# Attention's values divided by VectorE out of PSUM, in two halves of a pair

## The reference

```python
qkvg = x @ w_attn                                  # q 16 heads, k 8, v 8, gate 8
log_g = log_sigmoid(6.906768 + qkvg[..., QKV:])
q = _rope(q); k = _rope(k); k = repeat(k, 2); v = repeat(v, 2)
log_G = repeat(cumsum(log_g, axis=1), 2)
s = einsum('bthd,bshd->bhts', q, k) * scale
logits = 2 * log(abs(s) + 1e-30) + log_G[:, :, :, None] - log_G[:, :, None, :]
logits = where(tril, logits, -inf)
m = max(logits, axis=-1)
a = where(tril, exp(logits - m), 0)
num = einsum('bhts,bshd->bthd', a, v)
den = sum(a, axis=-1)
y = num / (den[..., None] + 1e-06)
y = (y - mean(y)) / sqrt(var(y) + 1e-09) * ln_w    # over the 64 of a head
attn = y.reshape(B, T, hq * d) @ w_proj
```

## Time and profile before

| | |
|---|---|
| median of 3 runs | 1180.68 us (1180.38 to 1182.2) |
| profiled execution | 1181.45 us, span 1179.7 us |
| busy: TensorE, VectorE, ScalarE, GpSimd | 1085.6, 927.7, 768.3, 678.2 us |
| mean granted TensorE clock | 0.984 of full speed |

### The profile page before, as it was taken

How to read it: one execution, slowest core, us unless ns; L and a number is a source line. 1 busy time by engine, 2 the same in 40 slices (tenths; PEclk the granted TensorE clock), 3 DMA queues, 4 the chain that set the end, 5 groups by cost and what they waited for, 6 DMA issues and landing times.

```text
span 1179.7 us, 23035 instructions
## 1 busy us (share of the span) xinstructions
PE 1085.6 (92%) x8367; PEld 790.3 (67%) x8367; DVE 927.7 (79%) x2046; ACT 768.3 (65%) x1630; POOL 678.2 (57%) x828
## 2 busy tenths in 40 slices
PE   3998788899999999999999999999999998999894
PEld 2665556566666777676767777777767676767663
DVE  6755856887878787878777787978798899998882
ACT  1323446676777786868687777877776677677751
POOL 0240508898988554554636373736577777877531
PEclk9999999999999999999999999999999999999997
DMA  8000101111111102020201111111111111112100
GB/s 226 1 1 1 31 10 51 38 33 32 30 29 45 44 22 74 19 77 19 68 26 43 36 53 44 53 44 28 36 43 42 53 53 49 53 35 68 35 8 18
DMA packets 40080, 49.33 MB, mean 42 GB/s; under 512 B 5631, under 2 KB 28157, under 8 KB 39968
## 3 DMA queue, kind: packets, MB, share of 16 engines
q1 hardware_dynamic: 35872, 42.33, 12.7%
q0 software_dynamic: 4096, 5.54, 1.7%
HBM read 33.15 MB, written 9.18 MB: 36 GB/s over the span
## 4 chain that ended last, share of the span: by engine, by line
PE 62%; POOL 16%; DVE 12%; issue 8%; ACT 1%; DMA 0%; POOLq 0%; SPq 0%; DVEq 0%; ACTq 0%
PE P L674 15%; PE P L644 15%; PE P L552 5%; POOL xe_d L1406 4%; PE P L605 4%; PE P L621 3%; POOL U L1353 3%; PE P L580 3%; PE P L595 2%; POOL U L1357 2%; POOL U L1399 2%; PE P L487 2%; PE P L490 2%; PE P L499 2%; PE P L587 2%
## 5 line engine op out<-in xcount | busy, mean ns | idle before, releaser
L644 PE MATMUL P<-Qt,Kt 64*128 64x256 f32 (+1 forms) x2560 | 293.9, 368 | 0.6 <-DVE U L1221 0.6
L644 PEld LDWEIGHTS P<-Qt,Kt 64*128 64x128 f32 x2560 | 218.7, 186 | 72.5 <-issue 53.8
L838 ACT ACTIVATE U<-P 128x512 f32<-128x512 f32 x384 | 207.5, 595 | 33.0 <-PE P L644 33.0
L674 PE MATMUL P<-U 128*64 128x256 f32 (+1 forms) x1792 | 195.0, 357 | 0.0
L835 ACT ACTIVATE U<-U 128x384 f32<-128x384 f32 x256 | 122.8, 524 | 70.9 <-DVE U L1221 70.8
L1221 DVE SCALAR_TENSOR_TENSOR U<-P,U 128x384 f32<-128x384 f32 x256 | 128.8, 550 | 49.4 <-PE P L644 42.4
L674 PEld LDWEIGHTS P<-U 128*64 128x64 f32 x1792 | 113.1, 137 | 69.4 <-issue 26.0
L1353 POOL TENSOR_TENSOR U<-U,consts 128x192 f32<-128x192 f32 x136 | 81.6, 623 | 131.1 <-ACT U L768 127.7
L1357 POOL TENSOR_TENSOR U<-U 128x384 f32<-128x384 f32 x128 | 134.3, 1049 | 35.2 <-DVE U L1204 19.3
L1251 DVE SCALAR_TENSOR_TENSOR P<-U,ES,P 128x512 f32<-128x512 f32 x192 | 144.3, 751 | 5.2
L1399 POOL TENSOR_TENSOR U<-U,SM 128x1024 f32<-128x1024 f32 x32 | 74.7, 2335 | 123.9 <-DVE SM L1285 123.7
(11 more groups left out here) (180 smaller groups left out, 2042.4 us busy)
## 6 DMA issues: line engine op xcount, KB each, us to landing
U<-H_d SPq DMA_DIRECT2D x32, 512.0 KB, 3.8
Kt<-Kt SPq DMA_DIRECT2D x64, 128.0 KB, 2.3
U<-in_w SPq DMA_DIRECT2D x21, 256.0 KB, 3.2
acc<-in_x SPq DMA_DIRECT2D x4, 512.0 KB, 5.9
out<-acc SPq DMA_DIRECT2D x8, 256.0 KB, 2.8
xe_d<-U SPq DMA_DIRECT2D x3, 448.0 KB, 7.0
U<-xe_d SPq DMA_DIRECT2D x7, 192.0 KB, 3.4
ye_d<-U SPq DMA_DIRECT2D x7, 192.0 KB, 5.1
```

The source lines that it names most:

```text
L644: mm = te.matmul(bank[:, 256 * n:256 * n + 256 - lo], Kt[u % 2][ki][rows, 128 * j:128 * j + 128], Qt[w // 2][rows, 256 * (w % 2) + lo:256 ...
L674: mm = te.matmul(P[3][64 * hd:64 * hd + 64, c + lo:c + 256], vt, A[s % NA][:, o:o + 256 - lo], start=i == 0 and n == 0, stop=i == m and n ...
L838: s.activation(A[n % NA][:, 512 * hd:512 * hd + 512], P[BANK["score", n, hd]][:, :], ACT.Square, scale=0.125, bias=GUARD).then_inc(a_sq, 1)
```

## The change

The quotient moves to VectorE and is made for each half of a pair as soon as its transposes are in PSUM. `quotient(p, i)` waits for the transposes, makes 1e-6 M + denominator for 8 columns straight out of PSUM, its reciprocals, and the product of the bank (128x512) with them, broadcast over 64 columns, into Y. ScalarE's copy (`y` in `ACT_AT`), VectorE's `sum` and GpSimd's `n1` are gone. The bank of `y` is free when the product is there (v_y instead of a_y); `ysq` waits for v_y of both halves. The wait for the transposes of the pair before last (p_fin), which protects Y, moves from ScalarE to VectorE. All four tables have new ticks.

```diff
--- before.py
+++ after.py
@@ -39,31 +39,31 @@
 FIRST = {154: ("proj", 0, 0), 158: ("proj", 0, 1), 162: ("proj", 0, 2), 166: ("proj", 0, 3),
          170: ("proj", 0, 4), 174: ("k", 0, 0), 175: ("proj", 0, 5), 179: ("proj", 0, 6), 181: ("q", 0, 0),
          183: ("proj", 0, 7), 188: ("k", 0, 1)}
-PE_AT = [(6.83, "max", 0), (12.46, "max", 1), (18.06, "max", 2), (23.8, "max", 3), (19.46, "y", 0), (24, "y", 1),
-         (39.58, "fin", 0), (39.63, "fin", 1), (49.26, "wp", 0), (51.14, "wp", 1), (-10.47, "q", 0), (-4, "q", 1),
-         (-21.13, "k", 0), (-8.63, "k", 1), (-35.49, "proj", 0), (-32.41, "proj", 1), (-28.75, "proj", 2),
-         (-24.06, "proj", 3), (-20.47, "proj", 4), (-18.24, "proj", 5), (-17.9, "proj", 6), (-13.43, "proj", 7),
-         (32.21, "xe", 0), (36.58, "up", 0), (38.96, "up", 1), (40.76, "up", 2), (41.81, "up", 3), (42.66, "up", 4),
-         (51.67, "up", 5), (52.15, "up", 6), (56.34, "up", 7), (65.22, "down", 0)]
-ACT_AT = [(11.04, "nt", 0), (23.94, "nt", 1), (2.41, "square", 0), (3.4, "square", 1), (4.26, "square", 2),
-          (5.7, "square", 3), (7.09, "square", 4), (8.41, "square", 5), (12.94, "square", 6), (14.33, "square", 7),
-          (16.65, "square", 8), (18.5, "square", 9), (-8.63, "decay", 0), (-5.21, "decay", 1), (-0.73, "decay", 2),
-          (6.93, "decay", 3), (-11.48, "q", 0), (-3.15, "q", 1), (-20.75, "k", 0), (-9.76, "k", 1),
-          (-34.56, "proj", 0), (-33.14, "proj", 1), (-29.92, "proj", 2), (-25.78, "proj", 3), (-20.15, "proj", 4),
-          (-17.77, "proj", 5), (-17.29, "proj", 6), (-13.75, "proj", 7), (20.21, "y", 0), (24.86, "y", 1),
-          (40.36, "fin", 0), (41.98, "fin", 1), (30.35, "ysq", 0), (35.25, "xe", 0), (39.38, "up", 0),
-          (39.75, "up", 1), (42.44, "up", 2), (43.47, "up", 3), (65.06, "down", 0)]
-DVE_AT = [(0.73, "scale", 0), (1.48, "scale", 1), (7.93, "scale", 4), (12.76, "scale", 6), (3.47, "top", 0),
-          (6.77, "top", 2), (8.54, "top", 3), (10.71, "top", 5), (16.85, "top", 7), (19.09, "top", 8),
-          (19.26, "top", 9), (7.19, "max", 0), (15.01, "max", 1), (18.36, "max", 2), (21.99, "max", 3),
-          (-32.86, "proj", 0), (-32.22, "proj", 1), (-28.81, "proj", 2), (-24.22, "proj", 3), (-20.89, "proj", 4),
-          (-18.87, "proj", 5), (-18.21, "proj", 6), (-12.51, "proj", 7), (49.88, "wp", 0), (52.69, "wp", 1),
-          (27.27, "sum", 0), (33.2, "var", 0), (34.24, "root", 0), (35.34, "root", 1), (36.12, "root", 2),
-          (44.36, "up", 4), (48.82, "up", 5), (53.22, "up", 6), (57.15, "up", 7)]
-POOL_AT = [(-1.06, "select", 0), (-0.11, "select", 1), (1.79, "select", 2), (7.81, "select", 3), (1.08, "vs", 1),
-           (5.63, "vs", 2), (12.62, "vs", 3), (-33.03, "proj", 0), (-31.21, "proj", 1), (-27.71, "proj", 2),
-           (-27.05, "proj", 3), (-19.68, "proj", 4), (-17.5, "proj", 5), (-15.98, "proj", 6), (-14.36, "proj", 7),
-           (27.65, "n1", 0), (33.73, "n2", 0)]
+PE_AT = [(6.74, "max", 0), (12.25, "max", 1), (22.1, "max", 2), (23.23, "max", 3), (16.08, "y", 0), (28, "y", 1),
+         (39.28, "fin", 0), (39.98, "fin", 1), (49.86, "wp", 0), (51.64, "wp", 1), (-10.01, "q", 0), (-2, "q", 1),
+         (-21.03, "k", 0), (-8.32, "k", 1), (-35.49, "proj", 0), (-32.41, "proj", 1), (-28.25, "proj", 2),
+         (-24.22, "proj", 3), (-20.74, "proj", 4), (-17.91, "proj", 5), (-17.9, "proj", 6), (-13.76, "proj", 7),
+         (32.69, "xe", 0), (36.67, "up", 0), (38.26, "up", 1), (40.05, "up", 2), (40.85, "up", 3), (42.67, "up", 4),
+         (50.96, "up", 5), (52.03, "up", 6), (55.22, "up", 7), (58.45, "down", 0)]
+ACT_AT = [(11.51, "nt", 0), (24.07, "nt", 1), (2.6, "square", 0), (3.02, "square", 1), (4.59, "square", 2),
+          (5.24, "square", 3), (7.09, "square", 4), (7.61, "square", 5), (11.93, "square", 6), (13.47, "square", 7),
+          (16.64, "square", 8), (16.75, "square", 9), (-9.28, "decay", 0), (-4.03, "decay", 1), (-2.36, "decay", 2),
+          (6.17, "decay", 3), (-10.72, "q", 0), (-1.17, "q", 1), (-19.89, "k", 0), (-9.74, "k", 1),
+          (-34.5, "proj", 0), (-33.96, "proj", 1), (-29.42, "proj", 2), (-26.15, "proj", 3), (-19.95, "proj", 4),
+          (-17.58, "proj", 5), (-16.9, "proj", 6), (-14.68, "proj", 7), (41.01, "fin", 0), (41.98, "fin", 1),
+          (30.24, "ysq", 0), (35.31, "xe", 0), (37.65, "up", 0), (40.88, "up", 1), (42.23, "up", 2),
+          (42.66, "up", 3), (58.27, "down", 0)]
+DVE_AT = [(-0.14, "scale", 0), (1.09, "scale", 1), (8.48, "scale", 4), (13.19, "scale", 6), (4.1, "top", 0),
+          (6.77, "top", 2), (8.54, "top", 3), (11.17, "top", 5), (16.73, "top", 7), (19, "top", 8),
+          (19.56, "top", 9), (7.15, "max", 0), (14.3, "max", 1), (21.1, "max", 2), (22.46, "max", 3),
+          (-32.88, "proj", 0), (-31.6, "proj", 1), (-27.2, "proj", 2), (-24.36, "proj", 3), (-20.89, "proj", 4),
+          (-18.83, "proj", 5), (-16.3, "proj", 6), (-12.2, "proj", 7), (49.28, "wp", 0), (52.75, "wp", 1),
+          (34.06, "var", 0), (34.56, "root", 0), (36.21, "root", 1), (36.23, "root", 2), (43.44, "up", 4),
+          (52.43, "up", 5), (54.35, "up", 6), (55.33, "up", 7), (17.9, "y", 0), (29.82, "y", 1)]
+POOL_AT = [(-0.53, "select", 0), (0.44, "select", 1), (3.56, "select", 2), (9.43, "select", 3), (2.58, "vs", 1),
+           (6.04, "vs", 2), (11.41, "vs", 3), (-32.44, "proj", 0), (-31.78, "proj", 1), (-28.21, "proj", 2),
+           (-27.53, "proj", 3), (-18.35, "proj", 4), (-16.81, "proj", 5), (-15.34, "proj", 6), (-14.94, "proj", 7),
+           (33.72, "n2", 0)]
 SCATTER_AT = [2 * c for c in range(64)]
 KEYS_AT, ROW_AT = (-20, -6), 8
 GATHER_AT = [n for n in range(432, NSTEP) if n % 6 in (0, 2)][:64]
@@ -258,16 +258,16 @@
             "p_s p_av p_q p_k p_proj p_max p_y p_fin p_wp p_xe p_up p_dn")
         a_wg, a_xth, a_ht, a_silu, a_wv, a_wh, a_wp, a_ex, a_hs, a_es, a_e1 = sems(
             "a_wg a_xth a_ht a_silu a_wv a_wh a_wp a_ex a_hs a_es a_e1")
-        a_sq, a_qh, a_kh, a_raw, a_v, a_d, a_nt, a_y, a_ysq, a_yt, a_xet, a_esilu, a_ye = sems(
-            "a_sq a_qh a_kh a_raw a_v a_d a_nt a_y a_ysq a_yt a_xet a_esilu a_ye")
+        a_sq, a_qh, a_kh, a_raw, a_v, a_d, a_nt, a_ysq, a_yt, a_xet, a_esilu, a_ye = sems(
+            "a_sq a_qh a_kh a_raw a_v a_d a_nt a_ysq a_yt a_xet a_esilu a_ye")
         v_z, v_wgl, v_st, v_ag, v_rs, v_xc, v_hn, v_xtl, v_gt, v_add, v_wl, v_hl, v_one = sems(
             "v_z v_wgl v_st v_ag v_rs v_xc v_hn v_xtl v_gt v_add v_wl v_hl v_one")
         v_ch, v_lg, v_na, v_z1, v_pre, v_lG, v_hc, v_ng, v_esd = sems(
             "v_ch v_lg v_na v_z1 v_pre v_lG v_hc v_ng v_esd")
         v_ro, v_oh, v_tot, v_cnt, v_is, v_ig, v_e1, v_gk = sems("v_ro v_oh v_tot v_cnt v_is v_ig v_e1 v_gk")
-        v_t, v_mx, v_cos, v_mred, v_f, v_wp, v_cmb, v_eg = sems(
-            "v_t v_mx v_cos v_mred v_f v_wp v_cmb v_eg")
-        g_hn, g_sin, g_rot, g_sel, g_n1, g_n2, g_vs = sems("g_hn g_sin g_rot g_sel g_n1 g_n2 g_vs")
+        v_t, v_mx, v_cos, v_mred, v_den, v_y, v_f, v_wp, v_cmb, v_eg = sems(
+            "v_t v_mx v_cos v_mred v_den v_y v_f v_wp v_cmb v_eg")
+        g_hn, g_sin, g_rot, g_sel, g_n2, g_vs = sems("g_hn g_sin g_rot g_sel g_n2 g_vs")
 
         BANK, BEFORE = bank_plan()
 
@@ -286,7 +286,7 @@
             if kind == "max":
                 return v_mred, 4 * i + job[2] + 1
             if kind == "y":
-                return a_y, 2 * i + job[2] + 1
+                return v_y, 2 * i + job[2] + 1
             if kind == "fin":
                 return a_yt, 2 * i + job[2] + 1
             if kind == "wp":
@@ -786,17 +786,10 @@
                     for i, rows in enumerate((slice(0, 64), slice(64, 128))):
                         kc = s.activation(Kt[u % 2][i][rows, 512 * half:512 * half + 512], P[BANK[job]][rows, :], ACT.Copy)
                     kc.then_inc(a_kh, 1)
-                elif kind == "y":
-                    p, i = job[1:]
-                    ac.wait_ge(p_y, 2 * p + i + 1)
-                    if p > 1:
-                        ac.wait_ge(p_fin, 2 * (p - 2) + 2)
-                    s.activation(Y[p % 2].rearrange("p (m w c) -> p w m c", m=2, w=2)[:, i],
-                                 P[BANK[job]].rearrange("p (m c) -> p m c", m=2), ACT.Copy).then_inc(a_y, 1)
                 elif kind == "fin":
                     p, half = job[1:]
                     ac.wait_ge(p_fin, 2 * p + half + 1)
-                    ac.wait_ge(v_f, 15 * p + 3)
+                    ac.wait_ge(v_f, 13 * p + 1)
                     s.activation(YT[p % 2][:, 512 * half:512 * half + 512], P[BANK[job]][:, :], ACT.Copy).then_inc(a_yt, 1)
                 elif kind == "xe":
                     e = job[1]
@@ -855,7 +848,7 @@
                 elif kind == "decay":
                     decays(p, i)
                 elif kind == "ysq":
-                    ac.wait_ge(g_n1, p + 1)
+                    ac.wait_ge(v_y, 2 * p + 2)
                     ac.wait_ge(p_wp, 2 * (p // 2))
```

(38 more changed lines are left out.)

## The result

The kernel got slower where the forecast was faster. Six runs of the changed kernel have a median of 1187.17 us (1184.44 to 1189.07), six of the kernel before 1181.45 (1180.38 to 1183.0): ratio 1.0043, 95% interval 1.0025 to 1.006. The forecast was 1168.3 us, 19 us less, and its range ended at 1180. The profiled execution took 1189.07 us, span 1187.3, at a mean granted clock of 0.973 (before 0.984).

The account below looks back on a forecast made before the run. GpSimd's queue was taken to bound the scatter stage, TensorE the expert stage, both TensorE and VectorE nearly full in the gather stage. Terms -8.5 - 1.5 + 0.5 + 0 - 1.0 - 1.9 = -12.4 us gave 1168.3 us, range 1160 to 1180.

Parts of the forecast that it names:

- New tables and banks: Whole kernel: later bank release and reordered TensorE work cost nothing while VectorE is punctual; expert stage 0.5 us, ends 0 and 3.
- The path from values to `fin` loses 1.9 us of GpSimd: Gather stage: dropping the first normalisation shortens this path by 1.9 us, set against VectorE's added 1.1 us a pair.
- Scatter stage -8.5: 180 to 350 us: five first normalisations of 2.0 us leave GpSimd's queue; 8.5 us gained, ends 4 and 16.
- rival 2: Only the tail gains, 1.9 us, as GpSimd then waits as long for raw copies and roots: 1178.8 us, chance 0.08.
- rival 3: Gather stage gains too, from TensorE's 8.6 us of waiting, and scatter reaches 13 us: 1155.8 us, chance 0.17.
- VectorE's load, gather stage 0: 810 to 1112 us: VectorE's added 1.1 us a pair against 2.2 us of waits; taken as 0, ends -8 and +11.
- 350 to 430 us, -1.5: Between scatter and expert stages: the second normalisation starts some 2 us earlier; 1.5 us gained, ends 0 and 3.
- Expert stage +0.5: 430 to 810 us: TensorE always busy, same work in another order; 0.5 us lost, ends 0 and 3.
- Last two pairs -1.0: After 1112 us: two waits for the second normalisation, 4.1 us together, shrink by 1.0 us, ends 0 and 3.
- Tail -1.9: Serial end of the kernel: `ysq` starts sooner after the last transposes; 1.9 us gained, ends 1.6 and 2.1, surest term.
- Rival 1: VectorE becomes the gather stage's bound, each quotient waiting 2.0 us for transposes: +35 us, 1203 us, chance 0.10 for slower.
- The two rules: Quotients, with one input in PSUM, are never stretched beside GpSimd; giving saturated VectorE's work to ScalarE, which the change reverses.

Follow-up runs that it names:

- the tenth run: The change with variance and the root's first step put back at their old VectorE ticks, second step left late: 1178.18 us, 0.9969 of the kernel before.
- the first: Quotients on VectorE as in the change, but in the tables of the kernel before, at ticks 20.3 and 25.0: 1217.12 us, 1.0288 of the kernel before.
- the fourth run: The change with the second half's transposes back at TensorE tick 24 and its quotient at VectorE tick 25.0: 1194.38 us, 1.0104 of the kernel before.
- the third: The change with variance and all root steps back at their old VectorE ticks: 1176.5 us, 0.9951 of the kernel before.
- the twelfth: Quotients on VectorE in the tables of the kernel before, at ticks 19.2 and 27.25 instead of 20.3 and 25.0: 1178.4 us, 0.9953 of the kernel before.
- the thirteenth: The change with eight unread identity transposes on TensorE ahead of its wait for `n2`, outside the expert stage: 1176.49 us, 0.9951 of the kernel before.
- the eighth: The kernel before with the maxima reduction moved ahead of the root's first step and the rotation product ahead of its second: 1188.85 us, 1.0051.
- fifteenth run: The change once more, unaltered, timed beside the kernel before: 1188.18 us (1183.72 to 1192.11), ratio 1.0048.

## Why the prediction was wrong

By medians the path from before to the change has three steps: 1182.4 to 1169.1 us when `n1`'s time goes; to 1178.4 when VectorE makes the quotients and ScalarE's copies and `sum` go; to 1187.2 with the new tables. The prediction has no term for the granted clock in any of them.

- *"New tables and banks"*, costed at nothing outside the expert stage, cost 8.8 us. This step failed, and it alone turned a gain of 4 us (0.9953) into the loss. The prediction looked at banks and at `y`, and not at VectorE's order around the root, though it names GpSimd's wait for the root and TensorE's for `n2`. Putting that order back gives 10.7 us: the first root step had moved from 34.24 to 34.56, the next pair's reduction from 35.01 to 34.30 (15.01 and 14.3, a period of 20 on), and so they had changed places. By the tenth run most of what it cost was pace of TensorE and not waiting. The edit was in the diff, and the row that would have warned, TensorE waiting 8.6 us for `n2`, was read as a gain to come.
- *"The path from values to `fin` loses 1.9 us of GpSimd"*: it lost 0.6. From a pair's second `nt` copy (means of the ten pairs of the gather stage) the squares start after 10.40 us instead of 11.51, but the variance after 14.63 instead of 14.60: it stands at its place in VectorE's queue, and the time gained became waiting for that place (3.18 us from the end of the squares to the variance instead of 2.04). `n2` ends after 21.85 us, before 22.44.
- *Scatter stage -8.5*: -3.0 and -1.7 in the two profiles of the change, -2.0 with `n1` simply left out. Its lower end (4 us: nothing is won where GpSimd waits for the root) was near the truth and its middle was not; the waits took 5.0 us of the 9.3 that GpSimd shed. That is rival 2's mechanism. Two pairs took 60.0 us (180.13 / 3), not 57.5 to 58. (The sum gives the stage an upper end of 16 us, rival 3 one of 13; its 1155.8 us hangs on the 13.)
- *VectorE's load, gather stage 0*. The work itself is confirmed: 301.19 against 301.28 us in the old tables. VectorE's busy time rose by 22.6 us over 32 pairs, 0.7 a pair against the 1.1 summed (two quotients are busy for 2.10 us, not 2.38, which counts the steps between instructions): 1.4 a pair in the expert stage ((312.54 - 295.62) / 12) and 0.3 in the gather stage ((272.40 - 269.51) / 10), so the stretch that goes is 0 in the one and about 1.1 in the other; 0.6 was a fair mean. But the price was booked as nothing against a gain that was not booked either. Without the quotients the stage gives 5.9 us; with them it gives none. All in all the quotients on VectorE cost 9.3 us.
- *350 to 430 us, -1.5*: +1.8 in one profile, +0.1 in the other, and -0.2 in the old tables. The wait for `n2` stayed (3.5 against 3.3 us).
- *Expert stage +0.5*: +0.5. TensorE has no idle time there.
- *Last two pairs -1.0*: -0.8 and -0.9 in the two profiles of the change.
- *Tail -1.9*: from transposes to `ysq` 1.95 us less, as worked out. The stage as a whole gave 1.2 to 1.5.
- *Rival 1* (0.10 for slower): the sign was right, the mechanism was not that of this change, whose quotients wait only once, in the tail. It is that of the first and the fourth run.
- *The two rules.* No product of a quotient was stretched (690 to 692 ns in 64), which agrees with the Trainium skill, "SBUF — State Buffer", Who interferes with whom, on instructions with one SBUF input. That section speaks of them outside the two-port modes, which the prediction left out; the root's first `tensor_scalar`, L1277 of before, with one SBUF input, took 158 to 806 ns, and the trace doesn't show its mode. The Trainium skill, "Perfetto Trace Analysis", Optimizing Scalar/DVE Operations, says that giving work to ScalarE may make sense when VectorE is saturated. Here the opposite, with VectorE busy for 89% of the gather stage, cost 9.3 us, which agrees in sign, though it is not the large loss of rival 1.

Two of the signs that the prediction lists did not come: VectorE's busy share in the gather stage is 88%, not 91 to 94, and `n2` is still TensorE's largest wait there (17.4 us).

What is shown and what is not. Shown: the places of the variance and the first root step make 9.0 us; filling TensorE's idle time ahead of `n2` gives as much, filling behind it costs 14; the kernel before does not react to the filling; and by the pages TensorE's idle time is 90.7 and 92.3 us with those 9.0 us and 90.3 without them, so they are hardly waiting. How the 8.8 us of the new tables divide is an estimate. TensorE's idle time is 90.7 and 92.3 us in the two profiles of the change and 87.5 in the old tables with quotients (1176.7 - 1089.2): 3.2 to 4.8 us of waiting. The rest of the 10.6 and 7.9 us between the profiles is busy time, 7.4 and 3.1 us. The time at 1.2 GHz is 64 and 52 us against 31, of which at most half, 10 to 17 us, is lost. By stage it is 13.7 us of the gather stage in both profiles of the change, 6.8 in the tenth run, 3.4 in the third, none in the twelfth and the thirteenth: half of the 13.7 is close to the 7.6 and 6.2 us by which the last two are shorter there. In the scatter stage the third run has as much of it as the change, 10.2 us, and is as long (180.12 against 180.13).

Open: why the place of the first root step changes the clock at all, as the tenth run has the clock of the kernel before with 39.8 us of waits; and why the same places in the eighth cost waits and no clock. Where exactly idle time falls seems to decide, but no run tells which place does.

## What to carry to other kernels

When an edit comes with new positions in in-order queues, compare each engine's order around the latest wait instruction by instruction, and try a swap ahead of that wait before pricing the work that is moved: here it weighed 9 us for an instruction of 0.68. Then compare TensorE's idle and busy time separately, as busy time that grows with the same instructions is no wait. An instruction that is ready sooner gains only if its successor's place in a queue is sooner too (the squares came 1.1 us earlier, the variance not at all). Time taken from one engine is worth what its next wait leaves of it (9.3 us shed gave 2.0), while of time added more is lost (2.6 us a pair cost 2.0). And if TensorE idles shortly and often, look at the granted clock behind the idle time, not only at its length.

## What the runs showed of the hardware that was not expected

- A wait of TensorE of about 2 us in a stretch where it is busy nine tenths of the time was followed by the lower clock: 16 matmuls in 3.19 us instead of 1.66. Not each such wait is: the tenth run has as many us of them and less of the lower clock. Eight transposes of an identity ahead of the wait kept it at 1.00 through the gather stage, though they compute nothing.
- Runs of one kernel follow their granted clock. Of ten of the change (fifteenth run) the fastest, 1183.72 us, had 0.980, the slowest, 1192.11 us, 0.970. Of 83 of the kernel before, those beside the experiments, the 14 with 0.980 or less took 1184.81 to 1187.85 us, the 41 with 0.984 or more 1180.18 to 1182.47: an unchanged program loses by it as much as this change did.
- A small VectorE instruction with one operand in PSUM took 150 to 161 ns, less than the 174 of the shortest of the same operation with both in SBUF (L1260 of before), which had 16 elements instead of 8. And taking 1.9 us of GpSimd's work a pair away, with nothing changed on VectorE, took 4.7 us off VectorE's busy time over the ten pairs of the gather stage and 7.1 over the six of the scatter stage.
